# A selective-scan kernel: cumulative sums read from PSUM, the order of decays and guards, and the slots of a ring of rows

## The reference, cut to what matters

```
delta  = softplus(delta @ dt_proj_w.T + dt_proj_b)
dA     = einsum('bld,dn->bldn', dt, A);  dB_u = einsum('bld,bld,bln->bldn', dt, u, B)
dA_cum = exp(reverse cumulative sum of dA, shifted by one)
xs     = cumsum(dB_u * dA_cum) / (dA_cum + 1e-12)
y      = einsum('bldn,bln->bld', xs, C)
```

## Time and profile before

| what | value |
|---|---|
| median of 3 runs | 5924.44 us (5920.06 to 5930.22) |
| profiled execution, own time | 5927.52 us |
| its span, first to last instruction | 5925.6 us |
| busy: PE, DVE, ACT, POOL | 5018.5, 4725.9, 4088.8, 4474.3 us |
| mean granted TensorE clock | 0.933 of full speed |

### The profile page before, as it was taken

The page is one execution under the profiler, slowest core; times in us unless marked ns, Lnnn a source line. Parts: engine busy times, 40 slices in busy tenths (PEclk is TensorE's granted clock), DMA queues, the critical chain, the costliest instruction groups (busy, mean ns, idle before and its releaser), DMA issues. The chain is left out here.

```text
span 5925.6 us, 50719 instructions
## 1 busy us (share of the span) xinstructions
PE 5018.5 (85%) x14640; PEld 2540.6 (43%) x14640; DVE 4725.9 (80%) x4047; ACT 4088.8 (69%) x6429; POOL 4474.3 (76%) x2136
## 2 busy tenths in 40 slices
PE   6888888888888888888797878787979797999999
PEld 2333333333333334334343434343434344556578
DVE  6998989998999999989898999999999992222235
ACT  4878788888787888878787878787878784111100
POOL 4999999999999899989898989998999992000000
PEclk9999899999999999989898989898989898999999
DMA  2444444444434343434443434443434442343346
GB/s 83 130 130 128 125 128 129 132 129 131 124 125 134 125 129 130 128 121 131 122 132 124 129 125 126 133 125 121 131 126 132 128 131 91 95 139 113 103 164 217
DMA packets 555605, 755.30 MB, mean 127 GB/s; under 512 B 124091, under 2 KB 272443, under 8 KB 553277
## 3 DMA queue, kind: packets, MB, share of 16 engines
q1 hardware_dynamic: 540765, 737.36, 39.9%
q10 hardware_dynamic: 14560, 14.68, 0.8%
HBM read 662.04 MB, written 89.82 MB: 127 GB/s over the span
## 5 line engine op out<-in xcount | busy, mean ns | idle before, releaser
L633 POOL TENSOR_TENSOR g_ring<-dtu,b_ring 128x1024 f32<-128x1024 f32 x1026 | 2512.2, 2453 | 362.8 <-DVE e_ps L985 330.3
L985 DVE TENSOR_TENSOR_SCAN e_ps<-e_ps,g_ring 128x1024 f32<-128x1024 f32 x1024 | 2345.0, 2290 | 171.1 <-ACT e_ps L784 157.6
L784 ACT ACTIVATE e_ps<-dt,a_neg 128x512 f32<-128x512 f32 x2050 | 1398.4, 682 | 707.1 <-DVE v_own L1007 470.9
L1141 PE MATMUL y_ps<-v_ring,ident 128*128 128x512 f32 x3088 | 1621.2, 634 | 245.1 <-DVE res_gate L968 200.0
L642 POOL TENSOR_TENSOR v_ring<-z_ring,c_ring 128x1024 f32<-128x1024 f32 x768 | 1825.1, 2377 | 0.0
L794 ACT ACTIVATE f_ring<-rsum,consts,a_neg_half 128x512 f32<-128x512 f32 x2050 | 1645.8, 803 | 0.8
L998 DVE SCALAR_TENSOR_TENSOR z_ring<-f_ring,e_ps 128x1024 f32<-128x1024 f32 x768 | 934.8, 1217 | 48.6 <-issue 0.9
L1141 PEld LDWEIGHTS y_ps<-v_ring,ident 128*128 128x128 f32 x3088 | 588.2, 204 | 889.2 <-issue 809.2
L1141 PE MATMUL y_ps<-v_own,ident 128*128 128x512 f32 x1028 | 535.2, 616 | 0.0
L1074 PE MATMUL side<-u,conv_diag 128*128 128x512 f32 x1088 | 493.7, 597 | 25.3 <-ACT disp_ring L745 18.6
L1311 ACT ACTIVATE x_act<-x_ps,x_bg 128x512 f32<-128x512 f32 x128 | 87.9, 687 | 570.8 <-PE x_ps L1370 570.8
(11 more groups left out here) (135 smaller groups left out, 5165.1 us busy)
## 6 DMA issues: line engine op xcount, KB each, us to landing
b_ring<-bc_scr SPq DMA_DIRECT2D x1027, 256.0 KB, 3.7
c_ring<-bc_scr SPq DMA_DIRECT2D x1025, 256.0 KB, 3.4
pT_scr<-rowT_ring SPq DMA_DIRECT2D x136, 256.0 KB, 4.0
m_pT<-pT_scr SPq DMA_DIRECT2D x16, 2048.0 KB, 8.8
sT_scr<-sT_ring SPq DMA_DIRECT2D x272, 64.0 KB, 2.9
x_xT<-sT_scr SPq DMA_DIRECT2D x16, 1024.0 KB, 9.3
eo_scr<-x_eo SPq DMA_DIRECT2D x32, 512.0 KB, 5.1
m_eo<-eo_scr ACTq DMA_DIRECT2D x14, 1024.0 KB, 7.4
```

Of the source, the lines that this page charges most:

```text
L633: pool.tensor_tensor(g_ring[:, k], dtu[d][:], both(b_ring[:, k:k + 1]), ALU.mult).then_inc(g_done, 1)
L784: act.activation(e_ps[:, i % 2, h], dt[d][:, h], ACT.Exp, scale=a_neg[:, d, c, n:n + 1]).then_inc(e_done, 1)
L985: dve.tensor_tensor_scan(e, e, g, 0.0, ALU.mult, ALU.add).then_inc(scan_done, 1)
L1141: pe.matmul(y_ps[:, t % 2], ident[:], v, start=(t % (TILES // PAIRS) < 2), stop=True, skip_group_check=True).then_inc(v_used, 1)
```

## The change

The pair of sums becomes two scans of 511 elements, one for each half, that read `dt` from SBUF and the softplus's own input from its bank of `side` in PSUM, as a lower bound that never takes effect (add, then max); `border` goes, and DVE frees the two banks instead of ACT. The sums, `dtu` and the cut come one, one and two tiles earlier. ACT issues both halves of a decay on even tiles, and on odd tiles both halves of a guard that is two steps ahead; `f_ring` gets a third slot. The slots of the ring reverse their order at steps 23 and 55 instead of at the end of a pass, and in steps 21 and 53 POOL's product goes ahead of its `inputs`. SP's side stores come two steps later and run over into the next pass.

```diff
-    FR = 2
+    F_AHEAD = 2
-    SP_LAG, X_STEP = 4, 19
+    SP_LAG, X_STEP = 6, 19
-    DTU_LAG, RSUM_LAG, CUT_LAG = 4, 4, 7
+    DTU_LAG, RSUM_LAG, CUT_LAG = 3, 3, 5
+    EARLY = (21, 53)
-    RING = [i % 3 for i in range(STEPS)]
-    RING[-1] = 1
+    RING = [0, 1]
+    while len(RING) < STEPS:
+        i = len(RING)
+        RING.append(RING[i - 2] if i - 2 in EARLY else 3 - RING[i - 1] - RING[i - 2])
...
-        f_ring = sb("f_ring", [P, FR, 2, L])
+        f_ring = sb("f_ring", [P, 3, 2, L])
-        border = sb("border", [P, 2 * L - 1])
...
+            def stores_of_step(b, i):
+                if b < 0:
+                    return
+                for t in (2 * i, 2 * i + 1):
+                    side_stores(At("loop", b, sp), t)
+                if i == STEPS - 1:
+                    store_rinv(At("loop", b, sp))
...
                     if i >= SP_LAG:
-                        for t in (2 * (i - SP_LAG), 2 * (i - SP_LAG) + 1):
-                            side_stores(at, t)
+                        stores_of_step(at.b, i - SP_LAG)
+                    else:
+                        stores_of_step(at.b - 1, STEPS + i - SP_LAG)
...
-                for t in range(TILES - 2 * SP_LAG, TILES):
-                    side_stores(at, t)
-                store_rinv(at)
...
             def dtu_of_pair(at, s):
-                for j in (s - 1, s):
-                    pool.wait_ge(side_free[at.bank(j)], at.freed(j))
+                pool.wait_ge(dt_done, 2 * at.pair(s))
                 pool.tensor_tensor(dtu[d][:], dt[d][:], u[d][:, i - 1:i + 1, PAD:], ALU.mult).then_inc(dtu_done, 1)
             def cut_chunks(at, s):
-                pool.wait_ge(rsum_done, at.pair(s))
+                for j in (s - 1, s):
+                    pool.wait_ge(side_free[at.bank(j)], at.freed(j))
                 pool.wait_ge(dtu_done, at.pair(s))
...
                 for i in range(STEPS):
-                    inputs(b, i + G_AHEAD)
+                    if i not in EARLY:
+                        inputs(b, i + G_AHEAD)
                     if i > 0 and not on_dve(i - 1):
                         times_c(b, i - 1)
+                    if i in EARLY:
+                        inputs(b, i + G_AHEAD)
...
-                        act.activation(dt[d][:, 0], side[:, at.bank(s - 1)], ACT.Softplus).then_inc(
-                            side_free[at.bank(s - 1)], 1)
-                        act.activation(dt[d][:, 1], src, ACT.Softplus).then_inc(free, 1)
+                        act.activation(dt[d][:, 0], side[:, at.bank(s - 1)], ACT.Softplus).then_inc(dt_done, 1)
+                        act.activation(dt[d][:, 1], src, ACT.Softplus).then_inc(dt_done, 1)
...
                 if i % N == 0 and h == 0:
-                    act.wait_ge(rsum_done, b * (NDIR * PAIRS) + (gi // N + 1))
+                    act.wait_ge(cut_done, b * (NDIR * PAIRS) + (gi // N + 1))
                 if h == 0:
-                    act.wait_ge(z_done, b * STEPS + (gi - FR + 1 + CR))
-                act.activation(f_ring[:, i % FR, h], rsum[d][:, h], ACT.Tanh,
+                    act.wait_ge(z_done, b * STEPS + (before(gi) + 1 + CR))
+                act.activation(f_ring[:, RING[i], h], rsum[d][:, h], ACT.Tanh,
...
                 for t in range(TILES):
-                    decay(b, t // 2 + 1, t % 2)
-                    guard(b, t // 2 + 1, t % 2)
+                    for h in range(2):
+                        if t % 2 == 0:
+                            decay(b, t // 2 + 1, h)
+                        else:
+                            guard(b, t // 2 + F_AHEAD, h)
...
-                        for j in (s - 1, s):
-                            dve.wait_ge(side_free[at.bank(j)], at.freed(j))
-                        sums, steps_ = halves(rsum[d]), halves(dt[d])
-                        last = 2 * L - 1
-                        dve.memset(sums[:, last:] if d == 0 else sums[:, 0:1], 0.0)
...
-                        dve.tensor_tensor_scan(out, data, turn, 0.0, ALU.add, ALU.mult).then_inc(rsum_done, 1)
+                        dve.memset(rsum[d][:, :, L - 1:L] if d == 0 else rsum[d][:, :, 0:1], 0.0)
+                        for h, j in enumerate((s - 1, s)):
+                            dve.wait_ge(dt_done, 2 * at.pair(s) - 1 + h)
+                            sums, steps_, raw = rsum[d][:, h], dt[d][:, h], side[:, at.bank(j)]
+                            if d == 0:
+                                out, data, least = sums[:, 0:L - 1][:, ::-1], steps_[:, 1:][:, ::-1], raw[:, 1:][:, ::-1]
+                            else:
+                                out, data, least = sums[:, 1:], steps_[:, 0:L - 1], raw[:, 0:L - 1]
+                            dve.tensor_tensor_scan(out, data, least, 0.0, ALU.add, ALU.max).then_inc(
+                                side_free[at.bank(j)], 1)
```

More of the change, by code:

```diff
@@ L808, in _ @@
                 decay(0, 0, h)
-                guard(0, 0, h)
+            for gi in range(F_AHEAD):
+                for h in range(2):
+                    guard(0, gi, h)
             for b in range(0, B, 1):
```

14 lines of the change are left out of this document (5 added, 9 removed).

## The result

The changed kernel takes 5844.78 us (median of 4 runs, 5838.37 to 5848.11) against 5927.33 us for the kernel before on the same chip: ratio 0.9853, 95% interval 0.9827 to 0.9879. It is faster, by 83 us where 192 were forecast, and lies outside the range. The profiled execution has a span of 5836.5 us. Its passes are (4821.3 + 3.5 - 91.1) / 16 = 295.9 us, against 301.7 before: 5.8 us a pass where 12.0 were forecast.

What follows compares the result with a forecast made beforehand. No engine is full; a pass is a sum of handovers and DVE sets the pace. Gross 18.4 us a pass, net 12.0, times 16 is 192 us, giving 5732 us, range 5645 to 5830.

Steps and rivals of the forecast that it cites:

- what is late next: The waits expected to appear once DVE's old ones go; they were to cut 18.4 us a pass to 12.0.
- Sums: DVE's sums at L926: freed from POOL's interference, a pair takes some 2.4 us; gain 6.3 us a pass.
- Ring: DVE's product of step 1 no longer waits for row C; gain 2.3 us a pass.
- Decays first: DVE's scans no longer wait for ACT's decays; gain all 9.85 us a pass, bounds 0 and 9.85.
- Pair 2: Tile 39: the first sum waits for the softplus and holds up scan 20; minus 1.1 us a pass.
- Steps 21 to 31: ACT and PE run without pause to step 29's reduction, where DVE waits; minus 1.9 us, between 0 and 3.
- Pair 3: Tile 70: DVE frees the bank later than ACT did, so PE's fill and `y_gate` come later; minus 2.4 us.
- POOL: From step 50, `dtu` waits for its softplus and POOL falls behind; minus 0.5 us, between 0 and 5.
- given back: Rival: ACT and PE give the decays' gain back, leaving 6.0 us a pass, 5828 us; chance 0.15.
- the rival named slower: Sums wait for the softplus, held banks queue PE's fills and ACT's copies; 3.5 us a pair, 5956 us; chance 0.05.
- Pairs 1 and 4: PE and ACT have slack at these two pairs of sums, so the held banks cost nothing; minus 0.
- The sums are not freed: Rival: dt and the result stay in SBUF, so pairs take 3.9 us; 5796 us; chance 0.08.

Runs made afterwards that it cites:

- e4: The changed kernel with the ring order of the kernel before and no early POOL products: 5852.88 us, ratio 0.9849.
- h3: g3 with the ring order of the kernel before and no early POOL products: 5747.95 us, ratio 0.9702.
- e3: The changed kernel with one half of a decay and of a guard each tile again, guards one step ahead: 5856.62 us, ratio 0.9856.
- g2: The kernel before with only the short sums from PSUM, DVE freeing the banks, at the old lags and in the old order: 6075.92 us, ratio 1.0240.
- h2: The changed kernel with sums, dtu and cut back at 4, 4 and 7 tiles behind their fill: 5906.50 us, ratio 0.9971.
- g3: The changed kernel with dtu one tile later, fills slots2, slots3 and in0 later, and POOL's norm refinement sooner: 5711.81 us, ratio 0.9625.
- e2: The changed kernel with both inputs of the short sums in SBUF and the banks freed by ACT: 5982.76 us, ratio 1.0079.
- f1: The changed kernel with five zero-weight products on PE before the fill slots2, to keep PE busy: 5800.89 us, ratio 0.9763.
- f3: The changed kernel with POOL's norm refinement at the end of step 12 instead of 13: 5802.38 us, ratio 0.9767.
- e1: The changed kernel with dtu one tile later, as before the change: 5802.68 us, ratio 0.9765.

## Why the prediction was right and wrong

The direction was right, and so was the gross gain, 18.4 us a pass forecast and 18.2 measured (6.1 + 2.3 + 9.85). The step that failed is the list of what is late next: it was to give back 6.4 us and gives back 12.4. Three of its terms carry the difference: nothing stood for PE and its clock at step 21 (2.85 us), 2.4 for `y_gate` (4.6), 0.5 for POOL (2.2).

- **Sums.** Right: 1.20 us each, 6.1 us a pass against 6.3, no long ones, and passes of one kind (295.2 to 297.0 us from the second on). By pair the sums took 6.7, 2.3, 3.6 and 3.1 us in the mean before, and each pair takes 2.4 now, so most of the gain is at pair 1 and none at pair 2. The 9.4 us that the forecast took for the new sums are not its own four pairs of 2.4, which make 9.6 as measured.
- **Ring.** The wait went. Its 2.3 us were counted as kept; in the changed kernel 1.8 of them are given back at steps 12 to 16 (e4), in the kernel with the norm moved none of it there (h3).
- **Decays first.** All waits for decays went, as forecast. But of their 9.85 us, those at steps 5, 20 and 51 (7.1 us) also leave with the old order, once the sums are a tile nearer (e3 against g2): two edits remove the same time, and neither can be told from the waits of before alone.
- **Pair 2.** The sum waits 0.92 us for the softplus where 1.1 were forecast. The step that failed is that nothing else followed: PE's in-projection waits for the held bank too, the clock falls, and step 21 waits 2.85 us more. Steps 17 to 21 are 1.2 us longer where the decay of step 20, less the 1.1 us given back, should have made them 2.3 shorter; the sum had nothing to gain here. That the bank is behind it, h2 shows (held a tile longer, 6.4 us) and g3 (the fill moved away from it, none); some 1.7 of the 2.85 us go with the clock.
- **Steps 21 to 31.** The reduction of step 29 waits 3.08 us, and steps 22 to 31 take 46.7 to 46.9 us in every kernel that leaves the fills there, whatever comes before, except e2 (49.2). The stretch is set by ACT and PE, as forecast; what it gives back is the 0.8 us of decays within it, not 1.9.
- **Pair 3.** The term was 2.4 us and the stretch 35 to 38 was to be about 1.2 us longer; it is 3.5 longer. The chain was right, bank, fill, `y_gate`. The term was mis-sized by the clock: after 2.74 us of idle time the fill takes 3.4 to 3.8 us in every pass, where it took 2.05 in 11 of 16 before, and 1.95 with PE kept busy (f1). The forecast read one pass, and that was one of the five in which the fill was slow and `y_gate` waited already; the wait measures 5.07 us, of which some 2.6 are the clock's by the estimate at f1.
- **POOL.** The failed step is "I find it arriving between 0.3 and 2 us before it is needed: minus 0.5". That looked at g and at DVE, and for g it held, though its 2.33 us are the shortest product and not the median of 2.36: after the first, no scan waits for g. What POOL has due first is not g but nine operations of 0.2 us of the norm, for which ACT waits: 2.2 us a pass at step 15 (f3, and e1 for the share of `dtu`, 1.1 us).
- **The rivals.** The time came out between "given back" (5828) and no gain, but by the mechanism of the rival named slower. It was priced at 1.1 and 2.4 us at two pairs; the two cost 3.8 (0.92 + 2.85) and 4.6. Pairs 1 and 4, put at nothing, cost nothing. "The sums are not freed" is refuted by the 1.20 us of every sum, and e2 shows that it is the operand in PSUM that frees them. SP's stores, put at 0, cost nothing: in the twelve passes no instruction of DVE waits for a row.

Net, from the forecast's 12.0 us, counted afterwards: the waits of step 15 cost 2.2 where 0.5 stood for POOL, step 21 costs 2.85 where nothing stood, `y_gate` 4.6 for 2.4, steps 22 to 31 only 0.8 for 1.9, the sum's wait 0.9 for 1.1, the row statistics of step 18 (for ACT) 0.5 for nothing, and the sums gained 0.2 less: 12.0 - 1.7 - 2.85 - 2.2 + 1.1 + 0.2 - 0.5 - 0.2 = 5.85, and 5.8 were measured. The close agreement is of waits read from the same trace and proves no term by itself; the terms for PE's and POOL's parts are those that experiments bear out.

## What to carry to other kernels

Whoever moves the release of a buffer from one engine to another must follow every queue behind it: the producer that waits for the buffer, what stands behind it on that engine, and the engine's clock after the idle time. A wait that disappears on an engine that is followed closely by another (POOL here) is also that engine's catching-up time; look at all that is due from it, the small operations for a third engine above all. Parts of a change should be priced together and tried apart: here the best part alone loses 2.4%, two parts remove the same waits, one loses, and moving some side work and `dtu` afterwards (g3, 133 us) brings more than the whole change did (83 us). Read a wait in all passes before pricing it from one, and look at TensorE's granted clock in the stretch where a small edit gains more than it should: half of what f1 brought came from a stretch that it does not touch, and half of what e1 brought went with the clock there too.
